# Stacked operands interleaved over every fourth row, and row maxima turned on VectorE, in a 16-sample transformer block

## The chip, the cores and the metric

The kernel runs on one core of one Trainium2 chip. The metric is the device time of one execution in microseconds. Most executions of a kernel agree within 0.3%; those of this one spread over about 1.2% (table below).

## The reference

The block is a PixArt layer over 16 samples of 256 tokens and 256 channels, 16 heads of 16 channels, everything in fp32:

```
x  = x + gate_a * (attention(modulate(ln(x))) @ W_proj + b_proj)
x  = x + cross_attention(q = ln(x) @ W_qc, kv = ln(ctx) @ W_kvc) @ W_cproj + b_cproj
x  = x + gate_m * mlp(modulate(ln(x)))          # 256 -> 1024 -> 256, gelu
attention: softmax(q k^T / 4) v, per head, 256 queries by 256 keys
```

The shifts, scales and gates come from one small product of the condition vector with W_mod.

## The kernel before

Each sample ("batch" b) passes through the two attentions (called x and y) and the MLP. The work is written as a software pipeline. A step t has a section A and a section B of 16 slots each. In A the heads of x of batch t are **scanned** (queries times keys, so that VectorE can take each query's maximum), while the heads of y of batch t-2 are **scored** (the same product again, keys by queries, with the maximum subtracted by an extra contraction row, then exponential on ScalarE). In B the heads of y of batch t-1 are scanned and those of x of batch t scored. All other work (projections, transposes, value products `pv_*`, MLP halves `up*`, `down*`) is placed behind a slot by a plan per engine, written out by hand: `SP_PLAN`, `PE_PLAN`, `ACT_PLAN`, `DVE_PLAN`, `POOL_PLAN`, entries of (task, batch shift, slot). Each engine works strictly in the order of its plan. In SP's plan only the order counts, since SP has no slots of its own. Semaphores carry every dependence between engines.

Queries and keys are split in a high and a low fp32r part, and the products hi*hi, hi*lo and lo*hi are made in one matmul with a stacked contraction: for each of two head parities, 3 parts of 16 channels stand one below another in rows 0 to 47 (and 64 to 111) of `QS` and `KS`. Row 48 (112) holds the negated maxima in `QS` and ones in `KS`. ScalarE (hi) and VectorE (lo) leave the projected q and k in `SQ` and `SK`, 128 rows; SP's transfers carry them into the stack: `stack` (L308) six transfers of 128 KB for k_x, k_y, q_x each; `half_stack` (L322) six of 64 KB for each half of the y queries, which wait for SQ_y and for the scores of the batch before (`QS_y` has one buffer). So a transfer reads 128 (64) rows of 1 KB and writes 16 neighbouring rows.

The maxima: L927 on VectorE reduces each scan to two columns of `MX`; per half of the heads TensorE transposes MX by the identity matrix (`maxima`, L563, two matmuls) into one of the two rotating banks, ScalarE copies it to `MT` (L754), and SP sends it into the stack (L328, one transfer of 8 KB). That is four times per batch: `max_x0`, `max_x1`, `max_y0`, `max_y1`. The scores of a half wait for that half's row (`s_row`); the scans of a half wait for the stacks (`s_load`). A scan also waits for the reduction two scans earlier, a score for the exponential two scores earlier. T_y (L525) turns the normalised input of the y queries; q_y (L544) needs both its parts, of which VectorE writes the low one (L835). T_m is the same for the MLP, with its norm on GpSimd (L416).

Of the kernel before, what the change touches and what calls it, by code (L numbers as in the profile page):

```python
# [26 lines left out]
    "A": [("gate_a", 0, 1), ("gate_m", -3, 4), ("max_y1", -2, 8), ("x_in", 2, 9), ("k_x", 1, 10), ("q_y0", -1, 12),  # L27
          ("max_x0", 0, 13), ("q_x", 1, 15), ("q_y1", -1, 15)],
# [14 lines left out]
    "A": [("up0", -3, 0), ("up1", -3, 0), ("max_y1", -2, 2), ("v_x", 0, 2), ("T_x", 1, 3), ("up2", -3, 5),  # L43
          ("k_x", 1, 6), ("up3", -3, 7), ("T_y", -1, 7), ("q_y", -1, 9), ("max_x0", 0, 9), ("q_x", 1, 13)],
    "B": [("max_x1", 0, 0), ("v_y", -1, 2), ("T_c", 0, 3), ("k_y", 0, 7), ("max_y0", -1, 8), ("T_m", -2, 12)],
# [3 lines left out]
          ("stats_y", -1, 5), ("norm_y", -1, 7), ("k_x", 1, 7), ("T_y", -1, 8), ("pt_y0", -2, 8), ("q_y", -1, 10),  # L49
# [10 lines left out]
BANKED = {"up0", "up1", "up2", "up3", "max_x0", "max_x1", "max_y0", "max_y1", "out_x", "out_y", "T_c", "T_y", "T_x",  # L60
          "T_m", "k_x", "q_x", "k_y", "q_y", "v_x", "v_y", "down0", "down1"}
HALVED = BANKED - {"T_c", "T_y", "T_x", "T_m", "max_x0", "max_x1", "max_y0", "max_y1"}
# [39 lines left out]
def build(nc, x, ctx_in, cond, bias, rows_in, bv_rows, wm1, wm2, wqk, wvx, wqc, wkvc, wo, wup, wdown, out):  # L102
# [8 lines left out]
    with es:  # L111
# [49 lines left out]
        MX = {s: sb(f"MX_{s}", [128, 2, NB, 2, PAIRS // 2], f32r) for s in "xy"}  # L161
        MT = [sb(f"MT{i}", [PAIRS, N], f32r) for i in range(2)]
# [26 lines left out]
        d_c = dram("d_c", (1, H))  # L189
        scan_bank = [es.enter_context(nc.psum_tensor(f"scan{i}", [128, 512], fp32)) for i in range(NSCAN)]  # L190
# [5 lines left out]
        s_ones = sem("s_ones")  # L196
        s_cond = sem("s_cond")
# [83 lines left out]
        def _(sp):  # L281
# [13 lines left out]

            def stack(which, s, b):

                src, dst, parts = {"q": (SQ[s], QS[s][b % 2], (HI, HI, LO)), "k": (SK, KS[s][b % 2], (HI, LO, HI))}[which]
# [3 lines left out]
                for part in (HI, LO):  # L302
                    if part == LO:
                        sp.wait_ge(s_lo[f"{which}_{s}"], b + 1)
                    for c in (c for c in range(3) if parts[c] == part):
                        for par in range(2):
                            row = 64 * par + HD * c
                            sp.dma_start(dst[row:row + HD, :, :].bitcast(fp32),  # L308
                                         src[:, part, par, :].bitcast(fp32)).then_inc(s_load[f"{which}_{s}"], 16)

            def half_stack(half, b):

                if half == 0:
                    sp.wait_ge(s_hi["q_y"], b + 1)
                if b >= 1:
                    sp.wait_ge(s_score_full, SCORES["y", b - 1] + PAIRS * (half + 1))
                for c, part in enumerate((HI, HI, LO)):
                    if half == 0 and part == LO:
                        sp.wait_ge(s_lo["q_y"], b + 1)
                    for par in range(2):  # L320
                        row = 64 * par + HD * c
                        sp.dma_start(QS["y"][b % 2][row:row + HD, 4 * half:4 * half + 4, :].bitcast(fp32),  # L322
                                     SQ["y"][64 * half:64 * half + 64, part, par, :].bitcast(fp32))\
                            .then_inc(s_load[f"q_y{half}"], 16)

            def maxima(s, half, b):
                sp.wait_ge(s_MT[s][half], b + 1)
                sp.dma_start(QS[s][b % 2][3 * HD:3 * HD + 65:64, 4 * half:4 * half + 4, :].bitcast(fp32),  # L328
                             MT[half][:, :].bitcast(fp32)).then_inc(s_row[s][half], 16)

# [43 lines left out]
            for t in range(FIRST, LAST + 1):  # L374
                if t == 0:
# [5 lines left out]
                    sp.dma_start(raw_up, wup).then_inc(s_raw[4], 16)  # L381
                if t == 1:
# [6 lines left out]
        def _(pool):  # L389
# [6 lines left out]
            nc.gpsimd.memset(KS["x"][0][:, :, :].bitcast(fp32), 1.0).then_inc(s_ones, 1)  # L396
# [95 lines left out]
        @block.tensor
        def _(pe):
# [65 lines left out]
            def maxima(s, half, b):  # L559
# [485 lines left out]
```

## Time and profile before

| what | value |
|---|---|
| median of 3 runs | 977.52 us (972.76 to 984.92) |
| span of the profiled execution | 980.9 us, 19308 instructions; its own time outside the span is not listed |
| TensorE busy, matmuls | 897.5 us (91%) |
| VectorE, ScalarE, GpSimd busy | 617.9, 590.5, 348.2 us |
| mean granted TensorE clock | 0.934 |
| DMA queue of SP | 42.3% of 16 engines' span |

The span runs from the first to the last instruction of the program. The granted clock is a share of 2.4 GHz and takes only the levels 1.2 and 2.4 GHz, so a mean between them says for how long each held.

### The profile page before, as it was taken

The numbers are of one execution on the slowest core, as the hardware profiler recorded it, in microseconds if no ns is written. First come the engines' busy times: TensorE is split into PE (matmuls) and PEld (weight loads), VectorE is DVE, ScalarE is ACT, GpSimd is POOL, SyncE is SP. The second block draws the span as 40 slices with busy tenths as digits, with TensorE's granted clock in tenths as the row PEclk, the third lists the DMA queues.
The fourth block names the chain that finished last, engine by engine and source line by source line (L and its number), as shares of the span: only waits on it lengthen the run. The fifth ranks groups of instructions, "written<-read, shape, count | busy, mean of one in ns | idle before, by whom it ended". The sixth has DMA issues, their size and how long they took to land.

```text
span 980.9 us, 19308 instructions
## 1 busy us (share of the span) xinstructions
PE 897.5 (91%) x7216; PEld 657.4 (67%) x7216; DVE 617.9 (63%) x1302; ACT 590.5 (60%) x1058; POOL 348.2 (35%) x398
## 2 busy tenths in 40 slices
PE   5487899999999999999999999999999999997967
PEld 4355566677776767676777767677777767665736
DVE  3437678767767776767767767577677776644220
ACT  2142556849585767667594948567684958482522
POOL 4604044326161615253342616153433524120212
PEclk9668789999999999999999979899999999798779
DMA  7774635363445363534436333735436361130001
GB/s 214 150 101 73 105 68 107 74 86 78 91 85 86 71 116 66 107 79 82 83 82 93 80 74 74 112 67 91 92 75 88 70 90 43 34 55 33 23 0 33
DMA packets 77311, 79.21 MB, mean 81 GB/s; under 512 B 9729, under 2 KB 71810, under 8 KB 76834
## 3 DMA queue, kind: packets, MB, share of 16 engines
q1 hardware_dynamic: 76930, 77.43, 42.3%
q8 instruction: 58, 0.95, 0.5%
q10 hardware_dynamic: 288, 0.54, 0.1%
q14 instruction: 35, 0.29, 0.1%
HBM read 22.82 MB, written 4.26 MB: 28 GB/s over the span
## 4 chain that ended last, share of the span: by engine, by line
PE 76%; DVE 6%; ACT 4%; DMA 4%; SPq 4%; issue 4%; POOL 2%; POOLq 0%; ACTq 0%; DVEq 0%
PE bank L544 18%; PE scan L640 14%; PE pv L596 12%; PE bank L583 11%; PE bank L554 6%; PE bank L574 5%; PE score L650 4%; PE bank L525 3%; SPq L322 3%; DVE MX_y L927 2%; PE bank L563 2%; DMA QS_y<-SQ_y 2%; ACT P L781 2%; DVE MX_x L927 1%; DMA QS_x<-SQ_x 1%
## 5 line engine op out<-in xcount | busy, mean ns | idle before, releaser
L781 ACT ACTIVATE P<-score 128x512 f32<-128x512 f32 x512 | 289.0, 595 | 202.2 <-PE score L650 197.9
L927 DVE TENSOR_REDUCE MX_y<-scan 128x2 fp32r<-128x512 f32 x256 | 168.3, 681 | 83.2 <-PE scan L640 82.8
L927 DVE TENSOR_REDUCE MX_x<-scan 128x2 fp32r<-128x512 f32 x256 | 170.8, 679 | 78.0 <-PE scan L640 78.0
L640 PE MATMUL scan<-KS_x,QS_x 48*128 48x256 f32 x512 | 121.4, 336 | 25.8 <-DVE MX_x L927 16.2
L467 POOL TENSOR_TENSOR y<-y,x_bias 128x256 f32<-128x256 f32 x32 | 23.3, 728 | 329.7 <-DVE y L895 329.7
L544 PE MATMUL bank<-xT_y,W 128*128 128x256 f32 x960 | 136.1, 292 | 2.3 <-DVE xT_y L835 1.7
L544 PEld LDWEIGHTS bank<-xT_y,W 128*128 128x128 f32 x960 | 121.8, 194 | 14.2 <-DVE xT_y L835 6.9
L583 PE MATMUL bank<-w_down,HH 128*128 128x256 f32 x512 | 129.5, 399 | 1.0 <-ACT HH L734 1.0
L640 PE MATMUL scan<-KS_y,QS_y 48*128 48x256 f32 x512 | 111.3, 327 | 19.8 <-DMA QS_y<-SQ_y 8.0
L650 PE MATMUL score<-QS_y,KS_y 49*128 49x256 f32 x512 | 116.8, 330 | 8.1 <-ACT P L781 6.3
L640 PEld LDWEIGHTS scan<-KS_x,QS_x 48*128 48x128 f32 x512 | 76.6, 196 | 68.9 <-issue 30.3
L640 PEld LDWEIGHTS scan<-KS_y,QS_y 48*128 48x128 f32 x512 | 74.0, 195 | 69.8 <-issue 54.7
L650 PE MATMUL score<-QS_x,KS_x 49*128 49x256 f32 x512 | 111.7, 328 | 1.5 <-ACT P L781 1.5
L583 PEld LDWEIGHTS bank<-w_down,HH 128*128 128x128 f32 x512 | 96.2, 197 | 19.3 <-ACT HH L734 1.2
L650 PEld LDWEIGHTS score<-QS_y,KS_y 49*128 49x128 f32 x512 | 74.3, 193 | 17.3 <-ACT P L781 13.7
L851 DVE STREAM_TRANSPOSE PT<-pv 128x512 f32<-128x512 f32 x64 | 45.4, 710 | 63.3 <-PE pv L596 63.3
L596 PE MATMUL pv<-P,V_y 128*32 128x256 f32 x1024 | 77.1, 424 | 1.5 <-ACT P L781 1.5
L650 PEld LDWEIGHTS score<-QS_x,KS_x 49*128 49x128 f32 x512 | 73.8, 195 | 5.3 <-ACT P L781 4.1
L596 PE MATMUL pv<-P,V_x 128*32 128x256 f32 x1024 | 71.1, 397 | 0.5 <-ACT P L781 0.5
L544 PE MATMUL bank<-xT_x,W 128*128 128x256 f32 x384 | 63.0, 312 | 3.2 <-POOL xT_x L429 3.2
L544 PEld LDWEIGHTS bank<-xT_x,W 128*128 128x128 f32 x384 | 53.1, 207 | 10.1 <-POOL xT_x L429 3.6
L734 ACT ACT_TABLE_LOAD x46 | 59.0, 1283 | 0.8
(109 smaller groups left out, 1316.7 us busy)
## 6 DMA issues: line engine op xcount, KB each, us to landing
KS_x<-SK SPq DMA_DIRECT2D x96, 128.0 KB, 4.3
QS_x<-SQ_x SPq DMA_DIRECT2D x96, 128.0 KB, 4.5
KS_y<-SK SPq DMA_DIRECT2D x96, 128.0 KB, 4.4
QS_y<-SQ_y SPq DMA_DIRECT2D x192, 64.0 KB, 2.6
x_in<-in_x SPq DMA_DIRECT2D x16, 256.0 KB, 2.7
c_in<-in_ctx SPq DMA_DIRECT2D x16, 256.0 KB, 2.9
gate_a<-d_gate SPq DMA_DIRECT2D x16, 256.0 KB, 3.4
gate_m<-d_gate SPq DMA_DIRECT2D x16, 256.0 KB, 3.5
```

The lines of the kernel that those rows point to most:

```text
L322: sp.dma_start(QS["y"][b % 2][row:row + HD, 4 * half:4 * half + 4, :].bitcast(fp32), SQ["y"][64 * half:64 * half + 64, part, par, :].bitca ...
L544: last = nc.tensor.matmul(to[:, i * N:(i + 1) * N], w[p][:, c, (blk + i) * 128:(blk + i + 1) * 128], xT[k][:, q, c, :], start=(n == 0), st ...
L554: last = nc.tensor.matmul(to[:, a * H:(a + 1) * H], xT[k][:, p, c, a * 128:(a + 1) * 128], w[q][:, c, c0:c0 + H], start=(n == 0), stop=(n ...
L574: last = nc.tensor.matmul(to[:, a * H:(a + 1) * H], OT[:, half, a * 128:(a + 1) * 128], w[:, half, :], start=(half == 0), stop=(half == 1))
L583: last = nc.tensor.matmul(to[:, 0:H], HH[:, c, a * 128:(a + 1) * 128], w_down[:, c, :], start=(c == 0), stop=(c == FB - 1))
L596: last = nc.tensor.matmul(pv_bank[half % NPV][32 * j:32 * j + 32, g * N:(g + 1) * N], V[s][:, kb, head_of(half, g, j), :], P[:, (4 * grp + ...
L640: scanned = nc.tensor.matmul(scan_bank[n % NSCAN][:, i * N:(i + 1) * N], QS[s1][b1 % 2][row:row + 3 * HD, p, i * 128:(i + 1) * 128], KS[s1 ...
L650: scored = nc.tensor.matmul(score_bank[s % 2][:, i * N:(i + 1) * N], KS[s2][b2 % 2][row:row + 3 * HD + 1, p, i * 128:(i + 1) * 128], QS[s2 ...
L734: last = nc.scalar.activation(HH[:, 2 * u + i, :], src[:, i * N:(i + 1) * N], ACT.Gelu_apprx_tanh, bias=bias_cols[:, col:col + 1])
L781: nc.scalar.activation(P[:, s % 8, :, :].rearrange("p a n -> p (a n)"), score_bank[s % 2][:, :], ACT.Exp, scale=SCALE).then_inc(s_exp, 1)
L851: nc.vector.transpose(PT[:, :, :, :].rearrange("p a b c -> p (a b c)"), pv_bank[half % NPV][:, :])\
L927: nc.vector.tensor_reduce(MX[s1][:, half, :, par, p], scan_bank[n % NSCAN][:, :].rearrange("p (a n) -> p a n", a=NB), AXIS.X, ALU.max, neg ...
```

## The change

The three parts of a channel go to rows c, c+4, c+8 and so on of the stack (c = 0, 1, 2), over all 128 rows, instead of three blocks of 16 rows per parity. Rows 3, 7, ... are zero, and the last of each half (63 and 127) carries the maxima in `QS` and ones in `KS`. The contraction has 63 rows for a scan and 64 for a score, where it had 48 and 49. One transfer carries one part and one half of the heads: 128 KB from 128 rows to 32 rows, each fourth. Weights and biases are reordered on the way in to suit (`by_half` for all four). k_x, k_y and q_x keep six transfers; a half of q_y now has three instead of six.

The maxima no longer pass through TensorE and ScalarE: a VectorE transpose of 32 x 32 squares turns `MX` (now 32 columns, 16 used) into `MT`, and four transfers with rows of 128 bytes each carry one half to the stack, instead of one with rows of 1 KB. In SP's order the maxima of x0 now come before q_y0, and q_y1 comes before q_x. The zeros need memsets at the start: two of 2048 columns on VectorE (first batch of x), five on GpSimd (two less of ones), and four small transfers for the rows of ones.

```
 SP_PLAN A: ... ("k_x", 1, 10), ("q_y0", -1, 12), ("max_x0", 0, 13), ("q_x", 1, 15), ("q_y1", -1, 15)
        ->  ... ("k_x", 1, 10), ("max_x0", 0, 11), ("q_y0", -1, 12), ("q_y1", -1, 13), ("q_x", 1, 15)
 PE_PLAN, ACT_PLAN: max_x0, max_x1, max_y0, max_y1 gone
 DVE_PLAN: + ("max_x0", 0, 7), ("max_x1", 0, 15) in A; + ("max_y0", -1, 7), ("max_y1", -1, 15) in B

 stack():
-  for par in range(2):
-      row = 64 * par + HD * c
-      sp.dma_start(dst[row:row + HD, :, :], src[:, part, par, :])
+  for half in range(2):
+      sp.dma_start(dst[c:c + 125:4, 4 * half:4 * half + 4, :], src[:, part, half, :])
 half_stack():
-  for par in range(2):
-      row = 64 * par + HD * c
-      sp.dma_start(QS["y"][b % 2][row:row + HD, 4 * half:4 * half + 4, :],
-                   SQ["y"][64 * half:64 * half + 64, part, par, :])
+  sp.dma_start(QS["y"][b % 2][c:c + 125:4, 4 * half:4 * half + 4, :], SQ["y"][:, part, half, :])
 maxima() on SP:
-  sp.dma_start(QS[s][b % 2][3 * HD:3 * HD + 65:64, 4 * half:4 * half + 4, :], MT[half][:, :])
+  rows = QS[s][b % 2][63:128:64, 4 * half:4 * half + 4, :].rearrange("r p (a i n) -> r (p a) i n", a=NB, i=4)
+  for i in range(4):
+      sp.dma_start(rows[:, :, i, :], MT[s][32 * i:32 * i + 2 * PAIRS, half, :])
 maxima() on VectorE (those on TensorE and ScalarE removed):
+  dve.wait_ge(s_scan_done, SCANS[s, b] + PAIRS * (half + 1))
+  wait(dve, s_row[s][half], 4 * 16 * b)
+  nc.vector.transpose(MT[s][:, half, :], MX[s][:, half, :]).then_inc(s_MT[s][half], 1)
 start:
+  VectorE: memset MX_x, MX_y (64 columns each), KS_x0, QS_x0 (2048 each) to 0, before the first silu step
+  GpSimd: memset KS_x1, QS_x1, KS_y0, KS_y1, QS_y0 to 0 (before: KS_x0, KS_x1, KS_y0, KS_y1 to 1)
+  SP: last_row(KS_x0) at t = -1, last_row(KS_x1, KS_y0, KS_y1) at t = 0
```

## Rows read from the trace of the kernel before

**Rows 1.** page: each engine's busy time, and the chain by line

```profile
PE 897.5 (91%) x7216; PEld 657.4 (67%) x7216; DVE 617.9 (63%) x1302; ACT 590.5 (60%) x1058; POOL 348.2 (35%) x398
...
PE bank L544 18%; PE scan L640 14%; PE pv L596 12%; PE bank L583 11%; PE bank L554 6%; PE bank L574 5%; PE score L650 4%; PE bank L525 3%; SPq L322 3%; DVE MX_y L927 2%; PE bank L563 2%; DMA QS_y<-SQ_y 2%; ACT P L781 2%; DVE MX_x L927 1%; DMA QS_x<-SQ_x 1%
```

**Rows 2.** windows, one batch each: length, busy us of PE, PEld, DVE, ACT, POOL; then PEclk

```profile
569.00:625.50 56.50, 54.34 (x456) 39.52 (x452) 39.00 (x83) 37.37 (x67) 21.17 (x24) 0.95 0.40 81
...
681.00:734.00 53.00, 51.42 (x450) 38.08 (x448) 38.39 (x81) 37.27 (x67) 21.17 (x24) 1.00 0.46 87
```

**Rows 3.** the chain of waits, us 430 to 440: start, us, what

```profile
438.42 0.32 PE bank L563 x2
```

**Rows 4.** timeline of PE, one full-clock batch: start, us, what, idle before it

```profile
507.24 1.70 PE L544 MATMUL bank<-xT_y,W 128*128 128x256 f32 x12
...
510.67 0.38 PE L650 MATMUL score<-QS_y,KS_y 49*128 49x256 f32 x1
...
515.64 0.35 PE L640 MATMUL scan<-KS_y,QS_y 48*128 48x256 f32 x1 [0.35 <-DMA QS_y<-SQ_y]
...
532.50 0.66 PE L525 MATMUL bank<-ident,xn_y 128*128 128x128 f32 x4
```

**Rows 5.** timeline of ACT, the same batch

```profile
509.79 0.36 ACT L754 ACTIVATE MT<-bank 8x256 fp32r<-8x256 f32 x1
510.05 1.76 ACT L781 ACTIVATE P<-score 128x512 f32<-128x512 f32 x3
```

**Rows 6.** timeline of DVE, the same batch

```profile
506.41 0.69 DVE L835 TENSOR_TENSOR xT_y<-bank,xT_y 128x512 fp32r<-128x512 f32 x1 [0.70 <-PE bank L563]
```

**Rows 7.** timeline of POOL, the same batch

```profile
529.94 2.43 POOL L416 TENSOR_SCALAR xn_y<-x,mv_m,rstd_m 128x256 f32<-128x256 f32 x2
```

**Rows 8.** timeline of SP, the same batch

```profile
503.07 3.79 SPq L308 DMA_DIRECT2D KS_x<-SK  x6
509.92 3.73 SPq L322 DMA_DIRECT2D QS_y<-SQ_y  x6
```

**Rows 9.** timeline of PE where two other batches pass from A to B

```profile
409.13 0.35 PE L640 MATMUL scan<-KS_y,QS_y 48*128 48x256 f32 x1 [1.39 <-DMA QS_x<-MT]
...
463.53 1.07 PE L596 MATMUL pv<-P,V_y 128*32 128x256 f32 x16 [0.48 <-ACT P L781]
```

**Rows 10.** page: DMA issues, KB each, median us to landing

```profile
QS_x<-SQ_x SPq DMA_DIRECT2D x96, 128.0 KB, 4.5
...
QS_y<-SQ_y SPq DMA_DIRECT2D x192, 64.0 KB, 2.6
x_in<-in_x SPq DMA_DIRECT2D x16, 256.0 KB, 2.7
```

**Rows 11.** one line's instructions: duration of an issue of L322, ns min/median/max

```profile
L322 SPq DMA_DIRECT2D QS_y<-SQ_y x192: 547/594/1920, 95.1 to 892.8; - x192
```

**Rows 12.** instruction groups: busy us, mean ns of one

```profile
L851 DVE STREAM_TRANSPOSE PT<-pv 128x512 f32<-128x512 f32 x64 | 45.4, 710 | 63.3 <-PE pv L596 63.3
...
L871 DVE STREAM_TRANSPOSE OT<-PN 128x256 f32<-128x256 f32 x64 | 27.5, 430 | 0.4
...
L396 POOL MEMSET KS_x<- 128x2048 f32 x1 | 1.8, 1804 | 0.0
```

**Rows 13.** timeline of SP, the start

```profile
18.77 3.91 SPq L308 DMA_DIRECT2D KS_x<-SK  x6
22.73 3.85 SPq L308 DMA_DIRECT2D QS_x<-SQ_x  x6
```

**Rows 14.** timeline of PE, the start

```profile
34.08 0.80 PE L640 MATMUL scan<-KS_x,QS_x 48*128 48x256 f32 x4 [9.14 <-DMA QS_x<-SQ_x]
...
57.50 0.59 PE L563 MATMUL bank<-ident,MX_x 128*8 128x128 f32 x2 [0.82 <-DVE MX_x L927]
...
101.56 0.55 PE L640 MATMUL scan<-KS_y,QS_y 48*128 48x256 f32 x1 [2.90 <-DMA QS_y<-SQ_y]
```

**Rows 15.** timeline of PE, near the end

```profile
891.60 0.77 PE L640 MATMUL scan<-KS_y,QS_y 48*128 48x256 f32 x2 [2.01 <-issue]
```

More of the change, by code:

```diff
@@ L26 @@
 SP_PLAN = {
-    "A": [("gate_a", 0, 1), ("gate_m", -3, 4), ("max_y1", -2, 8), ("x_in", 2, 9), ("k_x", 1, 10), ("q_y0", -1, 12),
-          ("max_x0", 0, 13), ("q_x", 1, 15), ("q_y1", -1, 15)],
+    "A": [("gate_a", 0, 1), ("gate_m", -3, 4), ("max_y1", -2, 8), ("x_in", 2, 9), ("k_x", 1, 10), ("max_x0", 0, 11),
+          ("q_y0", -1, 12), ("q_y1", -1, 13), ("q_x", 1, 15)],
     "B": [("max_x1", 0, 0), ("c_in", 1, 1), ("max_y0", -1, 4), ("k_y", 0, 4), ("out", -3, 4)],
@@ L42 @@
 ACT_PLAN = {
-    "A": [("up0", -3, 0), ("up1", -3, 0), ("max_y1", -2, 2), ("v_x", 0, 2), ("T_x", 1, 3), ("up2", -3, 5),
-          ("k_x", 1, 6), ("up3", -3, 7), ("T_y", -1, 7), ("q_y", -1, 9), ("max_x0", 0, 9), ("q_x", 1, 13)],
-    "B": [("max_x1", 0, 0), ("v_y", -1, 2), ("T_c", 0, 3), ("k_y", 0, 7), ("max_y0", -1, 8), ("T_m", -2, 12)],
+    "A": [("up0", -3, 0), ("up1", -3, 0), ("v_x", 0, 2), ("T_x", 1, 3), ("up2", -3, 5),
+          ("k_x", 1, 6), ("up3", -3, 7), ("T_y", -1, 7), ("q_y", -1, 9), ("q_x", 1, 13)],
+    "B": [("v_y", -1, 2), ("T_c", 0, 3), ("k_y", 0, 7), ("T_m", -2, 12)],
 }
@@ L59 @@
 }
-BANKED = {"up0", "up1", "up2", "up3", "max_x0", "max_x1", "max_y0", "max_y1", "out_x", "out_y", "T_c", "T_y", "T_x",
+BANKED = {"up0", "up1", "up2", "up3", "out_x", "out_y", "T_c", "T_y", "T_x",
           "T_m", "k_x", "q_x", "k_y", "q_y", "v_x", "v_y", "down0", "down1"}
-HALVED = BANKED - {"T_c", "T_y", "T_x", "T_m", "max_x0", "max_x1", "max_y0", "max_y1"}
+HALVED = BANKED - {"T_c", "T_y", "T_x", "T_m"}
 def within(b):
@@ L189, in build @@
         d_c = dram("d_c", (1, H))
+        ones = y[0:2, :, :].rearrange("p c n -> p (c n)")
         scan_bank = [es.enter_context(nc.psum_tensor(f"scan{i}", [128, 512], fp32)) for i in range(NSCAN)]
@@ L294, in _, with last_row @@
             sp.dma_start(raw_kvc, wkvc).then_inc(s_raw[3], 16)
+            def last_row(to):
+                return sp.dma_start(to[63:128:64, :, :].rearrange("r (a b) n -> r a (b n)", a=4).bitcast(fp32),
+                                    ones.unsqueeze(1).to_broadcast([2, 4, CB * N]))
             def stack(which, s, b):
+                if b == 0 and s == "x":
+                    sp.wait_ge(s_zero0, 2)
+                elif b < 2:
+                    sp.wait_ge(s_zero, 2 if s == "x" else 3 + b)
                 src, dst, parts = {"q": (SQ[s], QS[s][b % 2], (HI, HI, LO)), "k": (SK, KS[s][b % 2], (HI, LO, HI))}[which]
@@ L305, in stack @@
                     for c in (c for c in range(3) if parts[c] == part):
-                        for par in range(2):
-                            row = 64 * par + HD * c
-                            sp.dma_start(dst[row:row + HD, :, :].bitcast(fp32),
-                                         src[:, part, par, :].bitcast(fp32)).then_inc(s_load[f"{which}_{s}"], 16)
+                        for half in range(2):
+                            sp.dma_start(dst[c:c + 125:4, 4 * half:4 * half + 4, :].bitcast(fp32),
+                                         src[:, part, half, :].bitcast(fp32)).then_inc(s_load[f"{which}_{s}"], 16)
             def half_stack(half, b):
@@ L557, in values @@
                 return last
-            def maxima(s, half, b):
-                pe.wait_ge(s_scan_done, SCANS[s, b] + PAIRS * (half + 1))
-                to = take(f"max_{s}{half}", b)
-                for a in range(NB):
-                    last = nc.tensor.transpose(to[0:PAIRS, a * 128:(a + 1) * 128],
-                                               MX[s][:, half, a, :, :].rearrange("p b c -> p (b c)").bitcast(fp32),
-                                               ident[:, :])
-                last.then_inc(s_full, 1)
             def outputs(s, b, a, to):
@@ L721, in projected @@
                 if name == "q_y":
-                    wait(act, s_load["q_y0"], LOADS * b)
-                    wait(act, s_load["q_y1"], LOADS * b)
+                    wait(act, s_load["q_y0"], LOADS // 2 * b)
+                    wait(act, s_load["q_y1"], LOADS // 2 * b)
                 src = full(act, name, b)
@@ L746, in values @@
                     .then_inc(s_V[s], 1)
-            def maxima(s, half, b):
-                if s == "x":
-                    wait(act, s_row["y"][half], 16 * (b - 1))
-                else:
-                    act.wait_ge(s_row["x"][half], 16 * min(b + 2, B))
-                src = full(act, f"max_{s}{half}", b)
-                nc.scalar.activation(MT[half][:, :], src[0:PAIRS, 0:N], ACT.Copy).then_inc(s_MT[s][half], 1)
             tasks = {
                 **{f"up{u}": lambda b, u=u: up(u, b) for u in range(4)},
-                **{f"max_{s}{h}": lambda b, s=s, h=h: maxima(s, h, b) for s in "xy" for h in range(2)},
                 "T_y": lambda b: copied("T_y", "y", b),
@@ L872, in returned, with maxima @@
                     .then_inc(s_OT, 1)
+            def maxima(s, half, b):
+                dve.wait_ge(s_scan_done, SCANS[s, b] + PAIRS * (half + 1))
+                wait(dve, s_row[s][half], 4 * 16 * b)
+                nc.vector.transpose(MT[s][:, half, :], MX[s][:, half, :].bitcast(fp32)).then_inc(s_MT[s][half], 1)
             def out_x(b):
@@ L899, in _ @@
                    (("pt", turned), ("pn", normed), ("po", returned)) for s in "xy" for h in range(2)},
+                **{f"max_{s}{h}": lambda b, s=s, h=h: maxima(s, h, b) for s in "xy" for h in range(2)},
                 "out_x": out_x,
```

85 lines of the change are left out of this document (50 added, 35 removed), and 6 rows, old and new, of the table DVE_PLAN.

## The prediction, made before the changed kernel ran

> **What bounds the kernel now.** I read the page first. TensorE is busy 91% of the span, the next engine 63%, and the chain runs through TensorE lines for most of its length, with 2% on the transposes of the maxima (L563), 3% on the issues of the y queries (L322) and 2% on their landing [rows 1]. Those three lines are what the change touches, so the question is how much of each is really on the path.
>
> Next, the windows of one batch each. The thirteen from 147 to 840 us are alike but for clock and small waits: at the full granted clock (1.00, that is 2.4 GHz) a batch takes 53.0 us with 51.4 us of matmuls, and the worst one 56.5 us at 0.95 [rows 2]. The steady state is therefore a TensorE stream with 1.6 us of holes; a matmul taken out shortens the batch only if nothing else arrives just in time behind it. So I read the timeline of one batch engine by engine [rows 4 to 8] and asked at each removed step who is next.
>
> **Maxima off TensorE.** Each of the four pairs of transposes takes 0.32 us of the chain [rows 3]. 4 x 0.32 = 1.28 us per batch is the most that their removal gives. Step by step in that batch:
> - max_y1 (slot A1): what follows (v_x, T_x, up2, out_x, k_x) is a stream of matmuls to which ScalarE answers; no wait of it comes first. Gain 0.31.
> - max_x0 (slot A9): the next big step is q_y, which began at 507.24 us [rows 4], while VectorE's low part of its input ended at 506.41 + 0.69 = 507.10 [rows 6]. The wait for it was already as long as the transposes. VectorE waits for ScalarE's copy, which follows its table load and GELU and so hangs on k_x, 5 us earlier. Gain 0, bound 0.14.
> - max_x1 (slot B0): v_y, down0 and T_c follow, all fed long before. Gain 0.31.
> - max_y0 (slot B8): T_m, two slots later, began at 532.50 [rows 4]; GpSimd had ended its input at 529.94 + 2.43 = 532.37 [rows 7]. Of 0.31 only about 0.05 is won there, but the third scan behind it waited 0.17 us for the reductions, which do come earlier. Gain 0.2, bounds 0.05 and 0.31.
>
> **Maxima off ScalarE.** In A the copy at 509.79 pushed the exponentials to 510.05, and the score at 510.67 waited for the first of them [rows 4, 5]. Without the copy the exponential starts when the copy did, 0.26 to 0.36 us earlier; I take 0.3. The other three copies lie in holes of ScalarE.
>
> Sum per batch: 0.31 + 0 + 0.31 + 0.2 + 0.3 = 1.12 us; over 13 batches 14.6 us.
>
> **Maxima on VectorE.** A transpose of 512 columns takes 710 ns and one of 256 takes 430 [rows 12], so 1.09 ns per column and, for 32, about 185 ns (bounds: 0.1, if short ones lose the fixed part, and 0.43). Four per batch are 0.74 us on an engine that is 63% busy. Where each sits: max_x0 in A7 before the low part of k_x and the reduction of slot 8, in front of a VectorE idle of 0.70 us [rows 6]; max_y0 in B7 before that of k_y; max_x1 and max_y1 behind slot 15, before pn_y0, q_x, po_y0 and before stats_x, while TensorE has 1 to 3 us of other work until it needs the next reduction. Each waits also for the reduction just before it, its own engine's. Cost 0; uncovered, 0.74 us per batch.
>
> **The y queries.** Before, the transfers of q_y0 began at 509.92 and took 3.73 us to issue [rows 8], about 0.62 us each; the last one landed 2.4 us later, and the first y scan started at 515.64 after a wait of 0.35 [rows 4]. In other batches the wait was up to 1.43 us (1.39 in rows 9). Over the boundaries from 147 to 840 us the waits add up to 8.9 us: 0.34, 1.43, 0.35, 0.91, 0.75, 1.39, 0, 0.35, 0, 1.39, 0.34, 0.82, 0.82. Now three issues: the last begins at 509.92 + 1.24 = 511.2. How long it takes to land is the unknown of this change. Bounds: 2.4 us (64 KB took 2.6 in the median, and 256 KB over all rows 2.7 [rows 10]) and 4.5 (128 KB into 16 rows [rows 10]); I take 2.5, since the next paragraph puts the difference on the rows written. It lands at 513.7, 1.3 us before TensorE comes (515.29, less the 0.3 won above). But not the whole wait goes: behind the first slot of B stands pv_y3, which needs the exponential of A15; where no transfer was late it waited 0.48 us [rows 9], and at full clock it would wait 0.35 (a 0.6 us exponential against 0.43 us of matmuls, with handshakes). So each boundary gives its wait less 0.35: 1.08 + 0.56 + 0.40 + 1.04 + 1.04 + 0.47 + 0.47 = 5.1 us.
>
> **Why landing should be quicker.** At the start twelve transfers of 128 KB are queued from 18.77 us, and the first scan gets going at 34.08 after 9.14 us of waiting, although the last was issued by 26.6 [rows 13, 14]. 1.57 MB in 15.2 us, less 2.4 for one landing, is 123 GB/s, while SP issues 128 KB each 0.62 us, which is 211 GB/s. So something behind the queue limits them, and what these transfers share is that each writes only 16 neighbouring rows. The new ones write 32 rows spread over all 128. If they then keep up with SP, the last begins at 26.0 and lands at 28.5: 5.5 us won. The Trainium skill (SBUF — State Buffer, section on the DMA port swizzle) says that bandwidth goes by how many of 16 ports the rows reach, and that four neighbouring rows share one: 16 rows would reach 4 ports, each fourth row all 16. Its 27.2 GB/s per port make 109 GB/s; the trace has 123, so it agrees within the rough fixed part.
>
> **The rest of SP's queue.** Per batch it loses 6 issues and gains 12 for maxima, at 0.59 us [rows 11]. In A max_x0 (four) is now ahead of q_y0: k_x ends at 506.9 [rows 8], so 506.9 + 2.5 = 509.4, 0.5 before SQ_y is there. Cost 0. q_y1 is moved ahead of q_x: it waits for the last y score (515.0), q_x (six) and max_x1 (four) queue behind: 515.0 + 13 x 0.62 + 2.4 = 525.5, needed in slot B8 at about 530. Cost 0. max_y0 ahead of k_y delays a stack wanted half a batch later. x_in, gates and out keep their place.
>
> **Start and end.** The start gets 5.5 from the stacks. Two VectorE memsets of 2048 columns at 1.8 us (GpSimd's [rows 12]) to 2.2 (by the slope above) come before the silu steps, which began at 3.3: TensorE's first product moves by 0 to 1.1 us; I take -0.6. GpSimd's five memsets end before those of before did, as it waited for weights then. The boundary at 57.50 loses a wait of 0.82 and a slow pair of 0.59 [rows 14]; exponentials are next: +1.2. The y queries at 101.56 (wait of 2.90 [rows 14]; no pv_y3 behind) +2.6. The other transposes of the first two batches +1.0. Sum 9.7. At the end the last y queries had both halves, twelve issues, queued, and TensorE waited 2.01 us [rows 15]: +2.0; transposes at low clock +1.2, a copy +0.3. Sum 3.5.
>
> Total 14.6 + 5.1 + 9.7 + 3.5 = 33 us. Against the profiled span that is 980.9 to 948. The page gives no time outside the span, and the span lies within the runs, near the upper end; I take the saving from the median: 977.5 - 33 = **944.5 us**.
>
> **Rivals.**
> - *The spread rows don't help* (a limit per row of 1 KB read, which stays). For it: the rows read are the same. Against: 256 KB in 2.7 us [rows 10]. The 5.1 goes, so do 5.5 + 2.6 + 2.0, and the 0.3 of the copy in half the batches: 944.5 + 17 = 961.
> - *The gates eat more than I think*: only max_x1 and the copy count, 0.6 per batch: 944.5 + 7 = 951.
> - *Clock.* In 6 of the 13 windows the granted clock was below 1.00, about 7 us in all. Fewer holes could end that: 937. New holes before q_y and T_m could make every batch like the one of 56.5 [rows 2]: 3.5 more in 13 batches less those 7 is +38: 982, no change.
> - *SP becomes the bound*, the slower side. Place: four maxima issues ahead of q_y0. q_y0 is late once one of them takes over 1.1 us, since 506.9 + 4 x 1.1 + 1.24 + 2.5 = 515.0. An issue of L322 took 1.92 us once, 0.594 in the median [rows 11]. At 1.9 each, 3.2 us per boundary and 1.3 us for max_x1 in B8, over 15 batches: 944.5 + 68 = 1012. Against it: L328's own issues lie near 0.55. The Trainium skill (DMA: Bandwidth & Descriptors, Specifications) wants rows of 512 bytes and more, below which a transfer reads, modifies and writes; these have 128. It gives no price; a longer landing has 4 us of slack here, only a longer issue hurts.
>
> **How the numbers follow.** Forecast with small errors (938 to 949) 0.52; gates (949 to 957) 0.16; clock better (931 to 938) 0.11; rows don't help (957 to 964) 0.10; clock worse 0.06; SP 0.05. Range 931 to 961 leaves out under 2 in 10 and takes in the bounds of the unknown costs. 2%, about what a measurement of this kernel tells from no change, lies at 958 and 997: faster 0.79, same 0.16, slower 0.05.
>
> **What the new profile would show.** No L563, no L754. A VectorE transpose MT<-MX of 0.1 to 0.2 us, 64 of them. Stack transfers landing in about 2.5 us; no scan waiting for QS_y; pv_y3 waiting 0.3 to 0.5 for the exponential; about 0.3 us of idle before q_y for xT_y. The first scan at 28 to 30 us. Batches at full clock of 51.5 to 52 us. The prediction fails if the landings stay above 4 us, if issues of the maxima take over 1 us, or if the clock falls in most batches.

## The result, and the profile after

The changed kernel takes 935.3 us (median of 4 runs, 933.6 to 938.0), the kernel before 975.5 in the same series (4 runs, 972.8 to 984.9): a ratio of 0.956, 95% interval 0.951 to 0.962. Faster by 4.4%, inside the range of 931 to 961, and 9 us below the forecast of 944.5.

The device time of a run is 1.8 us more than its span in every run here. By that the profiled execution of before (span 980.9) took about 982.7 us, an estimate, 7 us more than the median, while the changed kernel's (933.3) lies at its median. So the profiles differ by 47.6 us and the medians by 40.2. What follows accounts for the 47.6; where the median execution of before is 7 us shorter isn't shown.

The page of the changed kernel, answering to [rows 1]: busy times, TensorE's granted clock in tenths by slice, and the DMA rows (queue; then issues with KB each and median us to landing, as in [rows 10]).

```profile
PE 856.6 (92%) x7088; PEld 641.2 (69%) x7088; DVE 629.2 (67%) x1370; ACT 571.2 (61%) x994; POOL 350.9 (38%) x400
...
PEclk9767999999999999999999999999999999997879
...
q1 hardware_dynamic: 79402, 77.50, 25.4%
...
QS_x<-SQ_x SPq DMA_DIRECT2D x96, 128.0 KB, 2.1
...
QS_y<-SQ_y SPq DMA_DIRECT2D x96, 128.0 KB, 2.1
```

TensorE has 40.9 us less to do, but 128 fewer matmuls can't make that (at most 16 x 1.28 = 20 us, by [rows 3]): the rest is the same work at a higher clock. A stack transfer of 128 KB lands in 2.1 us instead of 4.5, and one of the y queries, twice as large as before, in 2.1 instead of 2.6. The queue moves what it did before (77.4 MB, then 42.3% of the engines' time) in 25.4%.

Windows of one batch each, from one first y scan to the next (columns as in [rows 2]):

```profile
385.60:436.80 51.20, 49.85 (x444) 37.66 (x442) 38.42 (x84) 35.63 (x62) 21.13 (x24) 1.00 0.28 89
...
793.40:933.30 139.90, 116.52 (x744) 86.81 (x740) 48.80 (x105) 60.11 (x100) 29.96 (x34) 0.85 0.09 28
```

Before, they took 53.0 to 56.5 us by the windows of [rows 2]. Now every one between 232 and 744 us takes 51.25 to 51.27, at clock 1.00, with 1.4 us of holes. The timeline of TensorE in one of them and at the start:

```profile
29.17 0.78 PE L645 MATMUL scan<-KS_x,QS_x 63*128 63x256 f32 x4 [3.49 <-DMA QS_x<-SQ_x]
...
93.74 0.55 PE L645 MATMUL scan<-KS_y,QS_y 63*128 63x256 f32 x1 [0.93 <-DVE MX_x L936]
...
480.47 1.67 PE L559 MATMUL bank<-xT_y,W 128*128 128x256 f32 x12 [0.25 <-DVE xT_y L834]
...
483.35 0.38 PE L645 MATMUL scan<-KS_x,QS_x 63*128 63x256 f32 x1 [0.55 <-DVE MX_x L936]
...
488.96 0.42 PE L602 MATMUL pv<-P,V_y 128*32 128x256 f32 x4 [0.48 <-ACT P L780]
```

The wait for QS_y is gone (the y scan at 488.09 has none) and pv_y3's wait of 0.48 for the exponential, foretold at 0.3 to 0.5, is what remains of the boundary. The 0.25 before q_y is the wait that max_x0 used to fill. At the start the first scan comes at 29.17 instead of 34.08 [rows 14].

SP's timeline in that batch (start, us, what) and VectorE's new group:

```profile
476.29 3.79 SPq L316 DMA_DIRECT2D KS_x<-SK  x6
480.12 2.21 SPq L338 DMA_DIRECT2D QS_x<-MT_x  x4
483.12 7.00 SPq L330 DMA_DIRECT2D QS_y<-SQ_y  x6
490.23 3.77 SPq L316 DMA_DIRECT2D QS_x<-SQ_x  x6
```

```profile
L876 DVE STREAM_TRANSPOSE MT_y<-MX_y 128x32 f32<-128x32 f32 x32 | 6.8, 212 | 1.1
```

Four maxima issues take 2.21 us, 0.55 each, and are out 0.8 us before the y queries start: SP did not become the bound. (The 7.00 us of the y queries are two groups of three, the second of which waits for the last y score.) A transpose of 32 columns takes 212 ns.

Where the span's 47.6 us (980.9 to 933.3) went, from the starts of the first y scans of each batch in the two timelines: to the second of them 147.06 became 133.79, so 13.3; the thirteen batches after it 691.5 became 659.6, so 31.9; the tail 142.3 became 139.9, so 2.4. The prediction had 9.7, 19.7 and 3.5. The question is the 12 us in the batches.

### The profile page after: what moved, and what is told of

The parts are those of the page before. It is cut to its first block, busy times and chain, and to the rows that moved or that the text cites. A ratio compares the mean times of both kernels' runs of the same rounds, so it can differ in the third digit from the quotient of the medians.

```text
span 933.3 us, 19104 instructions
## 1 busy us (share of the span) xinstructions
PE 856.6 (92%) x7088; PEld 641.2 (69%) x7088; DVE 629.2 (67%) x1370; ACT 571.2 (61%) x994; POOL 350.9 (38%) x400
## 3 DMA queue, kind: packets, MB, share of 16 engines
q1 hardware_dynamic: 79402, 77.50, 25.4%
## 4 chain that ended last, share of the span: by engine, by line
PE 60%; ACT 18%; DVE 9%; POOL 7%; issue 4%; SPq 1%; DMA 1%; POOLq 0%; DVEq 0%; ACTq 0%
PE bank L559 13%; PE bank L589 12%; PE scan L645 12%; PE pv L602 7%; PE bank L569 6%; ACT P L780 5%; POOL xn_y L433 4%; ACT L742 4%; PE bank L580 4%; PE score L655 3%; PE bank L540 3%; ACT HH L742 3%; ACT L780 2%; DVE MX_x L936 2%; ACT SK L734 1%
## 5 line engine op out<-in xcount | busy, mean ns | idle before, releaser
L645 PE MATMUL scan<-KS_x,QS_x 63*128 63x256 f32 x512 | 117.5, 331 | 20.9 <-DVE MX_x L936 16.8
L655 PE MATMUL score<-QS_y,KS_y 64*128 64x256 f32 x512 | 114.0, 325 | 7.2 <-ACT P L780 7.2
L645 PEld LDWEIGHTS scan<-KS_x,QS_x 63*128 63x128 f32 x512 | 74.3, 192 | 66.0 <-DVE MX_x L936 30.3
L645 PE MATMUL scan<-KS_y,QS_y 63*128 63x256 f32 x512 | 105.6, 317 | 6.7 <-DVE MX_y L936 5.2
L645 PEld LDWEIGHTS scan<-KS_y,QS_y 63*128 63x128 f32 x512 | 71.7, 189 | 53.5 <-issue 36.8
L655 PE MATMUL score<-QS_x,KS_x 64*128 64x256 f32 x512 | 105.6, 318 | 1.5 <-ACT P L780 1.5
L655 PEld LDWEIGHTS score<-QS_y,KS_y 64*128 64x128 f32 x512 | 72.1, 189 | 15.0 <-ACT P L780 9.9
L602 PE MATMUL pv<-P,V_y 128*32 128x256 f32 x1024 | 71.2, 397 | 7.6 <-ACT P L780 7.6
L655 PEld LDWEIGHTS score<-QS_x,KS_x 64*128 64x128 f32 x512 | 71.7, 190 | 5.0 <-ACT P L780 3.5
```

The lines of the kernel that those rows point to most:

```text
L602: last = nc.tensor.matmul(pv_bank[half % NPV][32 * j:32 * j + 32, g * N:(g + 1) * N], V[s][:, kb, head_of(half, g, j), :], P[:, (4 * grp + ...
L645: scanned = nc.tensor.matmul(scan_bank[n % NSCAN][:, i * N:(i + 1) * N], QS[s1][b1 % 2][row:row + 63, p, i * 128:(i + 1) * 128], KS[s1][b1 ...
L655: scored = nc.tensor.matmul(score_bank[s % 2][:, i * N:(i + 1) * N], KS[s2][b2 % 2][row:row + 64, p, i * 128:(i + 1) * 128], QS[s2][b2 % 2 ...
```

## Experiments

**Stacks alone.** Before's maxima path (TensorE, ScalarE), its plans and its order on SP stay; the stacks lie in every fourth row.

```diff
-                        for par in range(2):
-                            row = 64 * par + HD * c
-                            sp.dma_start(dst[row:row + HD, :, :].bitcast(fp32),
-                                         src[:, part, par, :].bitcast(fp32)).then_inc(s_load[f"{which}_{s}"], 16)
+                        for half in range(2):
+                            sp.dma_start(dst[c:c + 125:4, 4 * half:4 * half + 4, :].bitcast(fp32),
+                                         src[:, part, half, :].bitcast(fp32)).then_inc(s_load[f"{which}_{s}"], 16)
```

> The new stacks alone, with the old plans, the maxima on TensorE and ScalarE and the old order on SP. Theory: the stacks give back the start (3.5 us net of the memsets, then 2 us at the first y queries), 5 us of waits at the boundaries and 2 us at the end, 13 us in all; and the low-clock stretches of the steady part, about 8 us, follow the long waits at the boundaries, so they go too: 975.5 - 21 = 954 us, batches at 52.6 us, clock 1.00 in nearly all. Rival: the clock has nothing to do with the boundaries: 975.5 - 13 = 962 us, with several batches at a mean clock of 0.94 to 0.97.

Measured: 953.4 us (947.5 to 956.2; before 984.9 beside it), ratio 0.970 (0.964 to 0.976). That is the theory's 954 us. The profiled execution (span 945.7) was the shortest of the four. Window of a batch:

```profile
392.40:444.87 52.47, 51.20 (x454) 37.97 (x450) 37.91 (x80) 36.85 (x66) 21.19 (x24) 1.00 0.28 87
```

Thirteen batches take 675.0 us: 16.5 less than before. In the seven that ran at clock 1.00 in both, the difference is 1.14, 0.62, 0.44, 1.09, 0.54, 0.54 and 0.53, together 4.9: the waits. The other six, below 1.00 before, give 11.6, of which one wait of 1.39 explains 1.0. So waits 5.9, clock 10.6, as far as this one profiled execution of before tells.

**Maxima alone.** VectorE's transposes and four transfers each, but stacks in 16 neighbouring rows and the old order on SP.

```diff
-                sp.dma_start(QS[s][b % 2][3 * HD:3 * HD + 65:64, 4 * half:4 * half + 4, :].bitcast(fp32),
-                             MT[half][:, :].bitcast(fp32)).then_inc(s_row[s][half], 16)
+                rows = QS[s][b % 2][3 * HD:3 * HD + 65:64, 4 * half:4 * half + 4, :].bitcast(fp32)\
+                    .rearrange("r p (a i n) -> r (p a) i n", a=NB, i=4)
+                for i in range(4):
+                    sp.dma_start(rows[:, :, i, :], MT[s][32 * i:32 * i + 2 * PAIRS, half, :]).then_inc(s_row[s][half], 16)
```

> The maxima on VectorE alone (rows 48 and 112 of the old stack, four transfers, the old order on SP). Theory: 1.4 us per batch and 3 us at the two ends, less what the waits for the y queries grow (0.3 us in half the batches), clock losses as before: 975.5 - 19 = 956 us, waits for QS_y of 0.5 to 1.8 us at most boundaries. Rival (the clock recovers through less work on TensorE): 947 us.

Measured: 1009.5 us (1006.7 to 1014.6), ratio 1.028 (1.020 to 1.036): slower, and my expectation of 956 (rival 947) missed. The waits of TensorE by releaser (us in total, times, longest), and SP's and TensorE's timelines at one boundary:

```profile
PE scan L630 <- DMA QS_x<-MT_x: 39.4, 15, 3.5
```

```profile
249.62 3.74 SPq L320 DMA_DIRECT2D QS_y<-SQ_y  x6
253.41 2.22 SPq L329 DMA_DIRECT2D QS_x<-MT_x  x4
```

```profile
256.91 0.35 PE L630 MATMUL scan<-KS_y,QS_y 48*128 48x256 f32 x1 [2.16 <-DMA QS_x<-MT_x]
```

The y queries fill the queue from 249.62; the four transfers for the x scores start behind them and are all issued only at 255.63, when TensorE has been waiting for 0.9 us. Before, one transfer stood in their place. The y queries themselves were not late: the last of the six landed at 255.15, 1.8 us before the scan. Windows around that boundary:

```profile
256.91:258.50 1.59, 1.59 (x22) 0.87 (x24) 1.20 (x3) 0.60 (x1) 0.00 (x0) 0.99 0.76 182
258.50:261.90 3.40, 3.40 (x17) 3.17 (x18) 2.00 (x4) 0.60 (x1) 0.00 (x0) 0.50 1.17 128
261.90:265.00 3.10, 3.10 (x20) 2.42 (x19) 0.84 (x2) 0.81 (x2) 0.00 (x0) 1.00 0.99 126
```

After the hole of 2.16 us TensorE ran at 2.4 GHz for 1.6 us, then at 1.2 (clock 0.50) for 3.4. Ten of the twelve low stretches between 140 and 800 us began 0.2 to 1.6 us behind such a hole.

**The old order on the new stacks.**

```diff
-    "A": [("gate_a", 0, 1), ("gate_m", -3, 4), ("max_y1", -2, 8), ("x_in", 2, 9), ("k_x", 1, 10), ("max_x0", 0, 11),
-          ("q_y0", -1, 12), ("q_y1", -1, 13), ("q_x", 1, 15)],
+    "A": [("gate_a", 0, 1), ("gate_m", -3, 4), ("max_y1", -2, 8), ("x_in", 2, 9), ("k_x", 1, 10), ("q_y0", -1, 12),
+          ("max_x0", 0, 13), ("q_x", 1, 15), ("q_y1", -1, 15)],
```

> The changed kernel with the old order on SP: maxima of x0 behind q_y0, q_y1 behind q_x. Theory that the order matters: the fourth transfer of x0's maxima starts about 3.4 us after SQ_y is there and lands 0.5 us after TensorE comes to slot B0, of which the wait of pv_y3 hides a part: 0.2 to 0.5 us per batch, 935.3 + 3 to 8 = 938 to 943 us. Rival: the order is free with the quick stacks: 935 us, batches at 51.25 us.

Measured: 937.9 us (937.1 to 938.7), ratio 0.955 (0.950 to 0.960). A gap of 0.23 to 0.26 us stands before nearly every y scan in the batches, the batch is 51.26 us as in the changed kernel (pv_y3 would have waited anyway), which is the rival's figure. SP and TensorE at one boundary:

```profile
434.88 1.82 SPq L330 DMA_DIRECT2D QS_y<-SQ_y  x3
436.74 2.21 SPq L338 DMA_DIRECT2D QS_x<-MT_x  x4
440.25 0.35 PE L645 MATMUL scan<-KS_y,QS_y 63*128 63x256 f32 x1 [0.25 <-DMA QS_x<-MT_x]
```

Here the four transfers start 1.86 us behind the first of the y queries, in the run of the maxima alone 3.79: three issues instead of six stand before them. The 1.93 us between these are nearly the whole difference between the two holes, 0.25 and 2.16. So the hole came from the number of issues ahead in the queue, and not from how quickly they land.

**The new order on the old stacks**, with the maxima on VectorE.

> The maxima turned on VectorE and the new SP order (max_x0 ahead of the y queries), but the old stacks of neighbouring rows with four transfers per part pair. The run of the maxima alone was slower (1009.5) with 2.1 to 3.5 us in front of the y scans of every batch. Theory: that hole comes from max_x0 queued behind the six q_y0 transfers with their 8 us of writing; with max_x0 ahead of them it goes, so the boundary gap is under 0.5 us, batches 51.3 to 52.5 us, and the time is 950 to 965. Rival: the slow old stack itself holds the boundary (now q_y0 and q_y1 land 1 us later behind the maxima, and the queue of short packets is behind the bulk of k_x), so gaps of 1 to 2.5 us remain, batches 53 to 55 us, 985 to 1005.

Measured: 967.3 us (965.3 to 968.7; before 981.3), ratio 0.987 (0.982 to 0.992), so a gain of 1.3%. Gaps of 0.4 to 1.7 us, batches of 51.5 to 55.0 between 194 and 721 us: at the near side of the rival's gap, the time just above the range of the theory. Two of its windows:

```profile
301.84:354.19 52.35, 50.00 (x440) 37.70 (x441) 38.74 (x86) 35.70 (x62) 21.10 (x24) 1.00 0.47 88
246.81:301.84 55.03, 53.08 (x441) 39.78 (x441) 37.89 (x83) 35.70 (x62) 21.09 (x24) 0.94 0.42 82
```

The same 440 or 441 matmuls are 3.08 us longer busy at 0.94: this is what the clock costs. The order is worth four points of the ratio on the old stacks (1.028 to 0.987) and none that can be measured on the new (0.955 with the old order, 0.956 with the new). On the old stacks a gap is left: at the start of the first window's batch the y queries' issues start at 295.70 us, the sixth begins at 298.89 and lands at 301.75, and the scan began at 301.84 after 1.01 of waiting. With three issues of 128 KB the last begins 1.26 us after the first, with six 3.2.

**Transfers by themselves.** A kernel that only copies inside SBUF and does none of the reference's work: groups of six transfers, each group waited for. "near" writes 16 neighbouring rows per transfer (the second time 32, half as wide), "each" 16 rows, every eighth (the second time 32, every fourth, half as wide), "half" 64 KB into 16 neighbouring rows, "short" four transfers of maxima, "long" one of 8 KB.

> Only SBUF to SBUF transfers, six at a time and then a wait, four rounds of each; x is copied to the output, nothing of the block is computed. near16: 128 KB into 16 neighbouring rows. each8: into 16 rows, each eighth. near32: into 32 neighbouring rows. each4: into 32 rows, each fourth. half64: 64 KB into 16 neighbouring rows. Theory (what limits is how the written rows lie): near16 needs 1.1 us a transfer, six of them 8 us to the last landing; each8, near32 and each4 go at SP's pace, 0.62 us a transfer, 5.5 to 6 us for six, though each8 writes 16 rows too. Rival (the number of rows written limits): each8 as slow as near16. The four short transfers of the maxima: 2.2 us to issue and 2 us to land, 3.6 to 4.2 in all, against 2.5 for the one old transfer; rival (rows of 128 bytes are slow): over 6 us.

SP's timeline (start of the first issue, us of issuing):

```profile
3.04 3.90 SPq L37 DMA_DIRECT2D near<-src  x6
11.14 3.77 SPq L37 DMA_DIRECT2D each<-src  x6
16.66 3.83 SPq L37 DMA_DIRECT2D near<-src  x6
23.40 3.77 SPq L37 DMA_DIRECT2D each<-src  x6
28.66 3.77 SPq L37 DMA_DIRECT2D half<-src  x6
34.20 2.33 SPq L37 DMA_DIRECT2D short<-narrow  x4
37.58 0.50 SPq L37 DMA_DIRECT2D long<-src  x1
```

From one group's start to the next: 16 neighbouring rows 8.1 us, 16 rows with every eighth 5.5, 32 neighbouring 6.7, 32 with every fourth 5.3; half the bytes into 16 neighbouring rows 5.5. The same number of rows and bytes, spread, saves 2.6 us, so it matters where the rows lie; twice as many neighbouring rows save 1.4, so their number matters too as long as they are neighbours. At 5.3 us, 3.8 of them issuing, SP is what limits. Four maxima transfers are issued and landed in 3.4 us, the one old transfer in 1.6 (2.5 expected): the split costs 1.7 us of the queue. The Trainium skill (SBUF — State Buffer, section on the DMA port swizzle) counts, by its mapping of rows to ports, 4 ports for 16 neighbouring rows, 8 for every eighth row or 32 neighbours, 16 for every fourth. The slowest group here has the fewest ports and the quickest the most, but the two with 8 ports differ by 1.2 us, which the count doesn't explain.

**What the removed transposes were worth.** The changed kernel with idle pairs of transposes put back, in A1 and B0, and in A9 and B8.

```diff
+            def dummy(name, b):
+                to = take(name, b)
+                for a in range(NB):
+                    nc.tensor.transpose(to[0:PAIRS, a * 128:(a + 1) * 128], ident[:, 0:PAIRS], ident[:, :])
```

> The changed kernel with two idle transposes (identity by identity, into the bank of the next user, whose product overwrites them) put back on TensorE at the places of max_y1 (slot A1) and max_x1 (slot B0). Theory: both places are on the path, 0.31 us each: batches of 51.25 + 0.62 = 51.9 us at full clock. Rival: ScalarE and the others set the pace there too, 51.25 to 51.5.

> The same pairs of idle transposes at the places of max_x0 (slot A9) and max_y0 (slot B8). Theory: before q_y TensorE waits 0.25 us for xT_y and before T_m 0.17 us for GpSimd's norm, and these waits hide the pairs: 51.25 + 0.06 + 0.14 = 51.45 us, and the two waits are gone. Rival: each costs its 0.31 us: 51.9.

```profile
445.05:496.93 51.88, 50.44 (x450) 37.79 (x447) 38.45 (x84) 35.62 (x62) 21.13 (x24) 1.00 0.27 88
```

```profile
443.38:494.96 51.58, 50.46 (x448) 37.79 (x446) 38.47 (x84) 35.73 (x62) 21.20 (x24) 1.00 0.28 89
```

In the first window, A1 and B0 cost 0.63 (0.62 forecast). In the second, A9 and B8 cost 0.33 (0.20 forecast): A is unchanged at 27.1 us from x scan to y scan, so A9 is free as said, and B8 costs its full 0.33. One execution each, 943.8 and 943.3 us, so only the batches of their traces are compared.

**VectorE loaded.** Four more transposes of 32 columns behind each of the maxima.

```diff
+                for i in range(4):
+                    nc.vector.transpose(MZ[:, i, :], MX[s][:, half, :].bitcast(fp32))
```

> The changed kernel with four more transposes of 128 x 32 (into a tile that nobody reads) behind each of the maxima on VectorE, 0.6 to 0.8 us at each of four places, 2.4 to 3.2 us per batch. Theory: VectorE's idle time hides one transpose everywhere; five of them overrun the 0.3 to 0.7 us before T_y in A7 and the reductions of slots B8 to B12, and the batch grows by 0.3 to 1.2 us, to 51.6 to 52.4. Rival (VectorE's work at these places is on the path): 51.25 + 2.4 = 53.7 us or more.

Batches 51.47 us (+0.21, where 0.3 to 1.2 was expected), 939.5 us once. Four more transposes at each place cost 0.2 per batch together, so a cost near 0 for one is right.

**Holes made on purpose.** Eight, then twelve small transfers ahead of q_y0 (the diff shows the eight).

```diff
+                    for i in range(8):
+                        sp.dma_start(d_extra[8 * b + i], ident[0:2, :]).then_inc(s_extra, 16)
```

> The changed kernel with eight small transfers (two rows of 512 bytes of the identity into unused DRAM) on SP's queue ahead of q_y0, about 0.5 us each. SP had 0.8 us free there and the stack 1.6 us of slack, so the y scans come 1.6 us late in every batch, 0.48 of it where pv_y3 waits anyway. Theory: a hole of 1.5 to 2 us at the boundary brings the low-clock stretches back in many batches, each worth 1.5 us and more: some batches at 52.4 us with clock 1.00, others at 54 and above with 0.94 to 0.97, and 960 us or more in all. Rival: the clock doesn't answer to such holes: all batches at 52.3 to 52.5 us, 953 us.

> The changed kernel with twelve small extra transfers (two rows of 512 B, about 0.55 us of issue each) ahead of q_y0 in every batch. Eight of them left gaps of 0.2 to 1.8 us in front of the y scans and a granted clock of 1.00. Twelve should move q_y0 by 2.2 us more, so gaps of 2.2 to 3.5 us, as in the run of the maxima alone. If gaps of this size are what lowers the clock, batches with them show 0.94 to 0.97 and last 54.5 to 57 us, span 985 to 1010. If the clock fell in that run for another reason (the DMA engines busy with the old stacks), it stays at 1.00, batches are 53.3 to 54.5 us, and the span is 965 to 980.

Eight: 943.0 us once; the gaps were mostly 0.2 to 0.6 us, four of 1.16 to 1.82, and the clock stayed at 1.00 between 140 and 790 us. I had made the holes too small: an extra transfer took 0.31 us to issue (eight in 2.51), not 0.5. Twelve: 977.7 us once, span 975.9, gaps of 1.4 to 3.0 us (2.2 to 3.5 expected). Windows of the twelve:

```profile
244.84:245.70 0.86, 0.86 (x12) 0.58 (x16) 0.77 (x3) 0.32 (x1) 0.00 (x0) 0.99 0.58 192
245.70:249.10 3.40, 3.40 (x23) 2.31 (x16) 1.78 (x4) 0.87 (x2) 0.00 (x0) 0.50 0.60 201
...
244.84:299.10 54.26, 51.49 (x440) 38.66 (x441) 38.13 (x84) 35.72 (x62) 21.09 (x24) 0.97 0.26 84
571.36:623.80 52.44, 50.02 (x440) 37.67 (x440) 38.29 (x84) 35.73 (x62) 21.09 (x24) 1.00 0.27 87
```

Of 13 holes above 0.9 us between 140 and 800 us, nine (1.5 to 3.0 us) were followed within 0.6 to 1.5 us by a low stretch of 3.4 us; four (1.4, 1.4, 1.7, 2.5) were not. The DMA engines were at 26 to 27% here, as in the changed kernel: so holes at this place bring the clock down with quick stacks too, and busy DMA engines aren't needed for it. A batch with such a stretch has 1.5 us more of busy TensorE. This fits the maxima run's clock too, and part of what this change gained. The hole of 1.82 us among the eight drew no low stretch while one of 1.52 among the twelve did, so the size of one hole doesn't decide alone. In the run with the new order on the old stacks all four low stretches of that time came within 2.0 us behind a hole of 1.4 to 1.7 us, and five boundary holes of 1.0 to 1.5 drew none.

In the kernel before, the thirteen batches hold 28.0 us at 1.2 GHz in five stretches. Two of them (at 196.1 and 626.2 us, 10.2 us together) began within 0.6 us of a hole of 1.4 us. The other three (at 458.9, 564.7 and 834.4 us, 17.8 us of the batches' time) had no hole over 0.55 us in the 2 us before them, and that of the window of 56.5 us in [rows 2] is one of these. What brought them, and why nothing like them stands between 232 and 744 us in any kernel with the new stacks, no run shows.

**Small moves beyond the change.** The memsets of VectorE moved behind the first weight's split; then with it pv_y3 from B0 to B1 and q_xa from A12 to A11.

```diff
-            for to in (KS["x"][0], QS["x"][0]):
-                nc.vector.memset(to[:, :, :].bitcast(fp32), 0.0).then_inc(s_zero0, 1)
...
+                    for to in (KS["x"][0], QS["x"][0]):
+                        nc.vector.memset(to[:, :, :].bitcast(fp32), 0.0).then_inc(s_zero0, 1)
```

> The changed kernel with only VectorE's two memsets of the first x stacks put behind the split of the first down weight. If those memsets (1.76 us each) are what made the first PE product 1.04 us later than before, it comes at 5.1 us again and the first y scan at about 92.7 instead of 93.74 us; the span is 932.3 instead of 933.3. If the first product is held by something else (a weight's landing), it stays at 6.1 us. A second possibility: the stacks of x are zeroed too late and the first x scan moves later than 29.17 us.

> The changed kernel with three small moves: PE's task pv_y3 from step B0 to B1, q_xa from A12 to A11, and VectorE's two memsets of the first x stacks behind the split of the first down weight. My account says that what is left in a steady batch of 51.25 us above its PE work is the 0.48 us in front of pv_y3 and about half a us more around q_y and the next scan, and that the late first product costs 1.0 us. Expected: batches 50.2 to 50.8 us, first product at 5.1 us instead of 6.14, median 918 to 926. The rival: the wait before pv_y3 only moves to the next consumer (v_y's banks, or the reader of P one step later), because VectorE and ScalarE need their time anyway: batches 51.2 to 51.5, and then the median is 933 to 937.

Memsets alone: the first product starts at 5.08 us instead of 6.14, the first scan at 28.11 instead of 29.17, but the first y scan at 93.78 (93.74), not at 92.7 as expected: the microsecond is lost again in the first batch, and why isn't shown. Span 927.7, one run at 929.5; the fifteenth batch's first y scan is level too (793.49 and 793.40), and the 5.7 us lie in a tail with the same program:

```profile
793.49:927.70 134.21, 110.29 (x744) 81.78 (x740) 48.68 (x105) 60.06 (x100) 29.91 (x34) 0.90 0.10 30
```

Against 0.85 and 116.52 of busy time for the same 744 matmuls above. So the tail's clock differs between executions by more than the 2.4 us measured against 3.5 forecast, and that term can't be judged.

All three moves: 929.6 us (927.4 to 932.1; before 981.3), ratio 0.949 (0.945 to 0.953). That is the lowest median, but the interval overlaps the changed kernel's (0.951 to 0.962). Batches are 51.09 us, only 0.17 shorter, where 50.2 to 50.8 (and 918 to 926 us in all) was expected: the rival's side. Timeline of its TensorE:

```profile
481.52 0.38 PE L645 MATMUL scan<-KS_x,QS_x 63*128 63x256 f32 x1 [0.59 <-DVE MX_x L936]
...
485.57 0.38 PE L645 MATMUL scan<-KS_y,QS_y 63*128 63x256 f32 x1 [0.55 <-DVE MX_x L936]
```

With pv_y3 gone from its place, the second y scan waits 0.55 for VectorE's maxima instead. So the hole that remains looks like one of the scan and its reduction.

## Why the prediction was right, and where it was off

- *Bound and direction.* Right: a stream of TensorE with small holes, and no new wait on SP or ScalarE, and on VectorE only the 0.25 before q_y, as said. The range held, but by its lower part: 935.3 lies in the band of a better clock (931 to 938, chance 0.11), not in that of the forecast (938 to 949, 0.52). Full-clock batches, foretold at 51.5 to 52, took 51.26.
- *Maxima, 1.12 per batch.* Measured 1.21 (52.47 to 51.26, stacks alone against all). A1, A9, B0 as said; max_y0, taken at 0.2 because GpSimd's input for T_m was close, is worth its full 0.33. Left for ScalarE's copy is 1.21 - 0.96 = 0.25 against 0.3; no run took the copy alone away, but the time from q_y to the next score, where it stood, fell from 3.43 (507.24 to 510.67 in [rows 4]) to 3.17 us. What VectorE's low part of xT_y waits for is ScalarE's copy of xT_y, as the prediction had it against the releaser named in [rows 6]: the changed kernel's trace names that copy. Over 13 batches 15.4 against 14.6 (the last one is shorter).
- *Waits at the boundaries, 5.1.* Measured 5.9; pv_y3's wait was as foretold.
- *The step that failed: the clock.* I had counted 7 us of low clock in the thirteen batches, named "fewer holes could end that: 937" as a rival with 0.11, and left it at zero in the sum. That was read too small: in five of the six windows below 1.00 TensorE's busy time alone is 9.9 us above the 51.4 of a full-clock batch. It was 10.6 us in the profiled execution, and all of it went: 5.9 + 10.6 + 15.4 = 31.9. The run with twelve extra transfers shows that holes at this place bring the clock down in most batches. But of the 28.0 us at 1.2 GHz only 10.2 stood behind such a hole, so the cause of the larger part stays open. Taking 10.6 off the forecast gives 934, within 1.5 us of the result, and that is partly luck: the profiled execution of before was 7 us longer than the median, and the start gave 3.6 us more than forecast, the tail 1.1 less.
- *Start, 9.7 against 13.3.* The first scan came 4.9 us earlier, the sum of 5.5 and -0.6 by the two terms (the first product was in fact 1.04 later, so the stacks gave 5.9). The y scan's wait fell from 2.90 to 0.93, 2.0 against 2.6. The maxima gave 1.3 of it (the second y scan at 135.10 in the run of the stacks alone) against 1.2 + 1.0. Those are 8.2; the other 5.1 came together with a higher clock, from 0.82 to 0.95 in the second batch. That the clock is their cause is argued, not tried.
- *Stacks.* Landing at 2.5, measured 2.1 (up to 3.6 for the third of the y queries). The reason given, rows in one place, is shown by the transfers by themselves. For the y queries in the batches the halved number of issues is worth more than the landing: the last one begins 1.9 us earlier and lands 0.3 us quicker (2.1 against 2.4). The rival "the spread rows don't help" is out.
- *The order on SP.* Costed at nothing, right with these stacks. What I had not seen is that the parts don't add: the ratios are 1.028 for the maxima alone, 0.970 for the stacks alone, 0.956 for all, where a product would be 0.997. Four issues instead of one behind the y queries are affordable with three issues before them (a hole of 0.25 us) and not with six (2.16).

## What to carry to other kernels

When a stall is removed from a TensorE stream, price the clock with it: take the low-clock stretches of the profile, see which begin just behind a hole (here of 1.4 us and more), and put their cost in the forecast if the holes go, or add it if holes of 2 us come. Take more than one execution for it, since the clock's share differs between them. Try each part of a bundled change in the queue order that it will have: count the issues that stand ahead of what is waited for; one transfer turned into four was harmless ahead of the bulk or behind three issues, and dear behind six. For many transfers into few rows, spread the rows over all partitions before counting bytes.

## What the hardware showed that I had not expected

- Holes of TensorE at one place in every batch (1.5 to 3.5 us) were followed within 2 us by 3.4 or 6.8 us at 1.2 GHz in most batches (10 of 12 in the run of the maxima alone, 9 of 13 with twelve extra transfers), while four of up to 1.8 us in the run with eight extra transfers were not.
- 16 spread rows are nearly as good as 32: 5.5 against 5.3 us for six transfers of 128 KB, 3.8 of them issuing, and 8.1 for 16 neighbours.
- A transfer of rows of 128 bytes is no dearer to issue (0.55 us) than one of 128 KB (0.63); an extra one from two rows took 0.31 (twelve in 3.71 us).
- A tail of one and the same program took 134.2 us in one kernel and 139.9 in another, with TensorE 6.2 us less busy at a mean clock of 0.90 against 0.85.
